# First batch's way into the second attention done row tile by row tile during its gather; value projections moved ahead of the expert phase

## What is computed

```python
x = x + deformable_attention(ctx, norm(x))      # layer 0: 5 sampled keys for each of 16 heads
x = x + experts0(norm(x))                       # 32 experts of width 96, 4 per token
x = x + attention(norm(x), ctx, ctx)            # layer 1: 16 heads of 8, 154 keys, normed, gamma, beta
x = x + experts1(x)                             # 8 experts of width 512, 2 per token, Sinkhorn gate
# attention: probs = softmax(q @ k.T / sqrt(8)); out = probs @ v
```

## Time and profile before

| what | value |
|---|---|
| median of 3 runs | 1001.43 us (1000.84 to 1005.4) |
| the profiled execution's own time | 1003.65 us |
| its span, first to last instruction | 1001.8 us |
| PE busy | 667.4 us, 67% |
| DVE busy | 626.8 us, 63% |
| ACT busy | 423.3 us, 42% |
| POOL busy | 379.5 us, 38% |
| granted TensorE clock, mean | 0.818 |

### The profile page before, as it was taken

One profiled execution on the slowest core, in us unless ns is written; L12 is line 12 of the kernel. 1 busy time (PEld: TensorE's weight loads), 2 busy tenths in 40 slices (PEclk: granted clock), 3 DMA queues, 4 the chain that ended last, 5 costly groups with the idle time before them and its releaser, 6 DMA issues.

```text
span 1001.8 us, 14210 instructions
## 1 busy us (share of the span) xinstructions
PE 667.4 (67%) x3975; PEld 409.8 (41%) x3975; DVE 626.8 (63%) x1579; ACT 423.3 (42%) x906; POOL 379.5 (38%) x345
## 2 busy tenths in 40 slices
PE   5796796687758350777785636787864221799991
PEld 2342352243224240577751313343432111687881
DVE  3678998868948887257533643777754667343443
ACT  2574966665748231344441213354431000344442
POOL 2313223544352388000016886174420000566641
PEclk9998998978979755699995767989865555899996
DMA  4786966554545022244423311000002000111114
GB/s 134 242 280 209 296 223 190 181 169 142 195 158 192 8 82 79 74 127 121 122 75 124 120 43 37 1 17 1 11 1 105 1 0 0 38 43 43 41 35 136
DMA packets 82471, 102.52 MB, mean 102 GB/s; under 512 B 11288, under 2 KB 66014, under 8 KB 82015
## 3 DMA queue, kind: packets, MB, share of 16 engines
q1 hardware_dynamic: 58334, 79.72, 24.9%
q0 software_dynamic: 6592, 13.51, 4.5%
q10 hardware_dynamic: 17472, 8.39, 2.9%
HBM read 81.92 MB, written 19.66 MB: 101 GB/s over the span
## 4 chain that ended last, share of the span: by engine, by line
PE 40%; DVE 29%; ACT 7%; issue 7%; POOL 6%; DMA 5%; another core or an unknown queue 3%; SPq 1%; ACTq 0%; DVEq 0%; POOLq 0%
POOL xs L584 4%; PE PS L1977 4%; DVE oh L1173 3%; PE PS L1955 3%; DVE nmx L1310 3%; PE PS L1960 3%; DMA oh<-index 3%; PE PS L1784 2%; PE PS L1686 2%; PE PS L1858 2%; PE PS L1681 2%; PE PS L1860 2%; PE PS L1886 2%; PE PS L1968 2%
## 5 line engine op out<-in xcount | busy, mean ns | idle before, releaser
L616 POOL DMA_INDIRECT yb<-ys,yrow x64 | 61.2, 956 | 139.7 <-DMA ys<-y 117.7
L584 POOL DMA_INDIRECT xs<-xn,row x64 | 78.1, 1220 | 32.2 <-issue 18.5
L1173 DVE TENSOR_SCALAR oh<-oh,pcol 128x2048 bf16<-128x2048 bf16 x80 | 75.3, 941 | 21.6 <-DMA oh<-index 20.5
L1681 PE MATMUL PS<-oh,T 128*128 128x512 bf16 x240 | 73.2, 418 | 19.7 <-ACT oh L773 19.2
L579 POOL TENSOR_TENSOR vv<-vv,coef 128x1280 f32<-128x1280 f32 x16 | 44.3, 2767 | 97.5 <-DVE coef L1157 88.5
L682 POOL DMA_INDIRECT xg<-xrows,tok x39 | 37.5, 961 | 108.2 <-DVE tok L1519 96.6
L1686 PE MATMUL PS<-oh,T 128*32 128x512 bf16 x960 | 75.3, 421 | 0.3 <-issue 0.3
L1695 PE MATMUL PS<-ident,gs 128*128 128x128 f32 x320 | 56.5, 303 | 26.5 <-ACT vv L794 22.3
L1310 DVE TENSOR_REDUCE nmx<-PS 128x4 f32<-128x616 f32 x64 | 48.9, 794 | 27.9 <-remote 18.5
L786 ACT COPY gs<-PS 128x512 f32<-128x512 f32 x80 | 46.0, 575 | 43.1 <-PE PS L1686 25.4
L772 ACT ACTIVATE oh<-oh,pcol 128x512 bf16<-128x512 bf16 x80 | 57.8, 722 | 14.3 <-DMA oh<-index 14.3
(11 more groups left out here) (372 smaller groups left out, 1777.7 us busy)
## 6 DMA issues: line engine op xcount, KB each, us to landing
oh<-index SPq DMA_DIRECT2D x80, 512.0 KB
oh<-index SPq DMA_DIRECT2D x80, 128.0 KB
x<-xs SPq DMA_DIRECT2D x96, 64.0 KB, 1.9
ys<-y ACTq DMA_DIRECT2D x48, 128.0 KB, 2.2
w0r<-in_w SPq DMA_DIRECT2D x8, 384.0 KB, 5.6
xs<-nil SPq DMA_DIRECT2D x8, 256.0 KB
wg1r<-in_wg SPq DMA_DIRECT2D x1, 2048.0 KB
wu1r<-in_wu SPq DMA_DIRECT2D x1, 2048.0 KB
```

The source lines that it names most:

```text
L584: pool.indirect_dma_start(xs[:], bass.IndirectOffsetOnAxis(ap=row0[:, QT * b + t, k:k + 1], axis=0), xn1[:, b % 2, t, :], None).then_inc(s ...
L616: pool.indirect_dma_start(yb[:, b % 2, t, k, :], None, ys[:], bass.IndirectOffsetOnAxis(ap=yrow0[:, QT * b + t, k:k + 1], axis=0))\
L1173: dve.tensor_scalar(main, main, pcol[:, 0:1], None, ALU.is_equal).then_inc(s["oh_main"], 1)
L1681: pe.matmul(o, T2[:, b % 2, p, n // NK, :], oh[:, slot, GH, :], start=(p == 0), stop=False, skip_group_check=True)
```

## The change

For batch 0 alone, norm, transpose and queries are no longer done once for the batch in slots -11 to -2 but once for each row tile, in a loop that each engine runs ahead of the slots. The loop of DVE takes in the additions of the gather. Each step of the loop works on 128 rows of all four groups: four query matmuls of 128x128, four `qhi`, four `qf`. Between them lie the maxima of groups 0 and 1 for the row tile before. The first score matmul of a group still waits for that group's turn. `x2_ready` is raised for batch 0 where the last tile has been added. The order of the first nine units of maxima is changed (`FIRST_UNITS`), that from the tenth on is not.

The main values of all four batches are made behind sampling, among `keys` 4 to 7, in banks 6 and 4. The tail values of batch 0 are made at pair 1 of the expert phase, and nothing at pair 4; those of batches 1 to 3 stay behind the phase.

```diff
-KV_EVERY, KV_FIRST = 3, 1
+TAIL_PAIR = 1
-KV_KINDS = ("values", "tail_values")
+VALUE_BANKS = (6, 4)
+FIRST_UNITS = [("max", _g, _t) for _t in range(QT) for _g in range(2)] + [("turn", 0, 0)]
+FIRST_UNITS += MAX_UNITS[len(FIRST_UNITS):]
+AHEAD = 2 * QT + 1
...
@@ ScalarE
-                keys((e - E0 // 2) // 4 + 4)
+                i = (e - E0 // 2) // 4 + 4
+                keys(i)
+                values(i - 4)
...
+            def first_rows(t):
+                act.wait_ge(s["var2"], t + 1)
+                logs.link(act.activation(NA.log[:, t:t + 1], NA.var[:, t:t + 1], ACT.Ln))
+                act.activation(NA.rstd[:, t:t + 1], NA.log[:, t:t + 1], ACT.Exp, scale=-0.5).then_inc(s["rs2"], 1)
+                act.wait_ge(s["side_ps"], SIDE["xn2T", 0, t] + 1)
+                act.copy(pnT[:, t * P:(t + 1) * P], PS[:, 4, 0:P]).then_inc(s["side_read"], 1)
...
+                act.wait_ge(s["side_ps"], SIDE["q", 0, t] + 1)
+                for g in range(NG):
+                    cols = slice(g * P, (g + 1) * P)
+                    last = act.activation(qhi[:, t % 2, cols], PS[:, 4, cols], ACT.Identity, bias=bmask[:, 0, g:g + 1], scale=pcol[:, 3:4])
+                last.then_inc(s["q_made"], 1)
...
@@ VectorE
-            for t in range(QT):
+            def first_rows(t):
...
                 dve.wait_ge(s["gathered%d" % t], 16 * K0)
...
+                if t == QT - 1:
+                    dve.sem_inc(s["x2_ready"], 1)
+                c.link(dve.bn_stats(NA.st[:, t, :], XR[:, t, :]))
+                c.link(dve.bn_aggr(NA.mv[:, t, :], NA.st[:, t, :]))
+                dve.tensor_scalar(NA.var[:, t:t + 1], NA.mv[:, t, 1:2], EPS, None, ALU.add).then_inc(s["var2"], 1)
+                dve.wait_ge(s["rs2"], t + 1)
+                dve.tensor_scalar(xn2[:, t, :], XR[:, t, :], NA.mv[:, t, 0:1], NA.rstd[:, t:t + 1], ALU.subtract, ALU.mult)\
+                   .then_inc(s["xn2_ready"], 1)
+
+            def first_queries(t):
+                dve.wait_ge(s["q_made"], t + 1)
+                rows = slice(t * P, (t + 1) * P)
+                for g in range(NG):
+                    cols = slice(g * P, (g + 1) * P)
+                    last = dve.scalar_tensor_tensor(out=qf[:, 0, g, rows], in0=PS[:, 4, cols], scalar=bqk1[:, 0, g:g + 1],
+                                                    in1=qhi[:, t % 2, cols].bitcast(F32), op0=ALU.add, op1=ALU.add)
+                last.then_inc(s["side_read"], 1)
...
-            for r in range(FRONT_FIRST, PERIOD * (B - 1) + BACK_LAST + 1):
+            ahead = list(enumerate(FIRST_UNITS))[0:AHEAD]
+            for t in range(QT):
+                first_rows(t)
+                if t:
+                    maxima(0, ahead[2 * t - 2:2 * t])
+                first_queries(t)
+            maxima(0, ahead[2 * QT - 2:])
+            for r in range(0, PERIOD * (B - 1) + BACK_LAST + 1):
...
@@ TensorE
                     if b == B - 1:
-                        for i in (3, 4, 5):
+                        keys(3)
+                        for i in (4, 5):
                             keys(i)
+                            values(i - 4)
...
             for i in (6, 7):
                 keys(i)
+                values(i - 4)
...
-                if m % KV_EVERY == KV_FIRST and m // KV_EVERY < len(KV_KINDS):
-                    values(0, m // KV_EVERY)
+                if m == TAIL_PAIR:
+                    tail_values(0)
...
+            def first_turn(t):
+                side("xn2T", 0, t)
+                pe.wait_ge(s["xn2_ready"], t + 1)
+                pe.transpose(PS[:, 4, 0:P], xn2[:, t, :], ident[:]).then_inc(s["side_ps"], 1)
+
+            def first_queries(t):
+                pe.wait_ge(s["side_read"], SIDE["xn2T", 0, t] + 1)
+                for g in range(NG):
+                    cols = slice(g * P, (g + 1) * P)
+                    last = pe.matmul(PS[:, 4, cols], wq1[:, cols], pnT[:, t * P:(t + 1) * P], start=True, stop=True)
+                last.then_inc(s["side_ps"], 1)
...
+            for t in range(QT):
+                first_turn(t)
+                if t:
+                    maxima(0, ahead[2 * t - 2:2 * t])
+                first_queries(t)
+            maxima(0, ahead[2 * QT - 2:])
```

More of the change, by code:

```diff
@@ L89, with units_at @@
 MAX_UNITS.append(("turn", NG - 1, 0))
+FIRST_UNITS = [("max", _g, _t) for _t in range(QT) for _g in range(2)] + [("turn", 0, 0)]
+FIRST_UNITS += MAX_UNITS[len(FIRST_UNITS):]
+AHEAD = 2 * QT + 1
+def units_at(b, j):
+    units = MAX_UNITS if b else FIRST_UNITS
+    return [(n, unit) for n, unit in enumerate(units) if n // 2 - 1 == j and (b or n >= AHEAD)]
 MAX_BANKS = (2, 6)
@@ L98 @@
 SIDE = {}
+for _t in range(QT):
+    SIDE["xn2T", 0, _t] = len(SIDE)
+    SIDE["q", 0, _t] = len(SIDE)
 for _r in range(FRONT_FIRST, PERIOD * (B - 1) + BACK_LAST + 1):
@@ L105 @@
         _q = _r - PERIOD * _b
-        if _q == -8:
+        if _b and _q == -8:
             SIDE["xn2T", _b, 0] = len(SIDE)
-        if _q in Q_SLOTS:
+        if _b and _q in Q_SLOTS:
             SIDE["q", _b, Q_SLOTS[_q]] = len(SIDE)
@@ L740, in keys, with values @@
                 last.then_inc(s["k_ev"], 1)
+            def values(b):
+                act.wait_ge(s["v_ps"], b + 1)
+                act.copy(V1[:, b], PS[:, VALUE_BANKS[b % 2], :]).then_inc(s["v_ev"], 1)
             def post(b, n):
@@ L913, in _ @@
                     if q == -10:
-                        deviation(NA, "2", b + 1)
+                        deviation(NA, "2", QT + b)
                     if q == -8:
@@ L1291, in _, with maxima @@
                                                     in1=XR[:, t, :], op0=ALU.mult, op1=ALU.add)
-                    if t < QT - 1 or k < K0 - 1:
-                        c.link(last)
-                if t < QT - 1:
-                    c.tick(dve.bn_stats(NA.st[:, t, :], XR[:, t, :]))
-            last.then_inc(s["x2_ready"], 1)
-            def maxima(b, j):
-                for n, (kind, g, t) in enumerate(MAX_UNITS):
-                    if n // 2 - 1 != j:
-                        continue
+                    c.link(last)
+                if t == QT - 1:
[14 more added lines that the diff above has]
+                last.then_inc(s["side_read"], 1)
+            def maxima(b, units):
+                for n, (kind, g, t) in units:
                     u = N_MAX * b + n
+                    most = nmx if b or g != 1 else nmx1
                     bank = MAX_BANKS[u % 2]
@@ L1321, in split_query @@
                 u = NG * b + g
-                if b == 0:
-                    dve.wait_ge(s["q_made"], g + 1)
-                    dve.scalar_tensor_tensor(out=qf[:, 0, g, :], in0=PS[:, 4, :], scalar=bqk1[:, 0, g:g + 1],
-                                             in1=qhi[:, u % 2, :].bitcast(F32), op0=ALU.add, op1=ALU.add).then_inc(s["side_read"], 1)
-                    return
                 dve.wait_ge(s["side_read"], SIDE["q", b, g] + 1)
@@ L1625, in keys, with values @@
                 last.then_inc(s["k_ps"], 1)
+            def values(b):
+                if b >= 2:
+                    pe.wait_ge(s["v_ev"], b - 1)
+                bank = PS[:, VALUE_BANKS[b % 2], :]
+                pe.matmul(bank, cx[:, b, 1:1 + P], wv1[:], start=True, stop=False)
+                pe.matmul(bank, vrow[:, 1:1 + P], bv1[:], start=False, stop=True).then_inc(s["v_ps"], 1)
             def post(b, n):
@@ L1795, in _ @@
             for b in range(1, B):
-                for n in range(len(KV_KINDS)):
-                    values(b, n)
+                tail_values(b)
             def side(*use):
@@ L1872, in _ @@
                         scores(b, q // 3, q % 3)
[L1873 removed]
+                    maxima(b, units_at(b, q - MAX_FIRST - 1))
                 for b in range(B):
                     q = r - PERIOD * b
[L1876 removed]
+                    if b and q == -8:
                         side("xn2T", b, 0)
[L1878 removed]
+                        pe.wait_ge(s["xn2_ready"], QT + b)
                         for t in range(QT):
@@ L1881, in _ @@
                         last.then_inc(s["side_ps"], 1)
-                    if q in Q_SLOTS:
+                    if b and q in Q_SLOTS:
                         g = Q_SLOTS[q]
```

97 lines of the change are left out of this document (37 added, 60 removed).

## The result

| | before | changed |
|---|---|---|
| median of 20 runs | 1004.23 us (997.22 to 1013.28) | 1011.91 us (1004.23 to 1018.07) |
| ratio to before | | 1.0069, 95% interval 1.0044 to 1.0094 |
| profiled execution, own time | 1003.65 us | 1018.07 us |
| its span | 1001.8 us | 1016.2 us |
| PE, DVE busy | 667.4, 626.8 us | 674.1, 624.2 us |

The change makes the kernel slower by 0.7%, some 7.7 us of the medians. The forecast was +16.7 us, so the direction and the range held, and the forecast size was more than double the measured one. The profiled execution of the changed kernel is the slowest of its 20, so the 14.4 us between the two spans overstate the difference.

The account below looks back on a forecast made before the run. No engine was full; a chain of waits bound it, with POOL's batch 1 gathers behind x2_ready setting slot 1. +17.6 (rounds) - 0.9 (values) = +16.7 us: 1020.3 against the profiled 1003.65, 1018 on the median's scale; range 1007 to 1023.

Parts of the forecast that it names:

- The mechanism: Batch 0 to slot 1: DVE's rounds delay x2_ready, POOL's 30.2 us follow, DVE waits; each us later costs one.
- The gather's loop: DVE's loop over batch 0's tiles: rounds of 9.9, 11.4 and 11.4 us, making x2_ready 17.6 us later.
- 0.28 + 2.01 + 3.0 = 5.3 us: PE's part of a round: one tile's turn 0.28, four maxima matmuls 2.01, four query matmuls with tail 3.0 us.
- The clock: PE in the rounds: granted clock taken as 0.50 throughout; full clock would make the sum about 7 us smaller.
- The rival with the full clock: PE at full clock in the rounds: 6.8 us less, 1011 us; chance 0.2.
- What follows: Behind x2_ready: batch 1 ready at 591.9, slot 1 moves by the full 17.6 us, everything behind in the same order.
- The rival of the long stall: DVE's unexplained 11.24 us idle at 593.73 may vanish in a shifted kernel: 1007 us; chance 0.13.
- The values: Value projections moved behind sampling and to pair 1: expert phase shortened, together -0.9 us.
- The cover behind sampling: Main values delay PE by 2.3 us there, hidden by 7.2 us before the first expert tile: cost nothing.
- worth nothing: Behind the expert phase, beside the gather: three main-value blocks vanish from PE and ACT, with no gain.

Follow-up runs that it names:

- run 3: Changed kernel, but POOL starts batch 1's gathers once batch 0's transfers have landed, awaiting x2_ready only before its last addition: 1010.82 us, ratio 1.0066 to before.
- run 4: Kernel before with POOL's gathers of batch 1 started when batch 0 has landed: 1001.94 us, ratio 0.9989.
- run 7: Changed kernel with DVE's loop reordered, adding each tile as it lands before looking at the previous tile's queries: 1001.85 us, ratio 0.9963 to before.
- run 12: Changed kernel again, unedited, for a second profile: 1008.13 us, ratio 1.0082 to before.
- run 5: Kernel before with batch 2's gathers spaced, pairs each held for a count of mx_used: 991.43 us, ratio 0.9867.
- run 6: Kernel before with batch 2's sixteen gathers kept back to back but held until 16 units of maxima are used: 997.86 us, ratio 0.9942.
- run 1: Kernel before with only the value projections moved as in the change: 1003.08 us, ratio 1.0005.
- run 2: Changed kernel with the value projections back in their old places, the row-tile loop alone: 1019.71 us, ratio 1.0109 to before.
- run 9: Kernel before with gathers of batches 2 and 3 meant to be spaced; twelve of batch 3's sixteen stayed back to back: 985.56 us, ratio 0.9869.
- run 10: Changed kernel with the same spacing edit for gathers of batches 2 and 3: 1001.85 us, ratio 1.0014 to before.

## Why the prediction was right in sign and range, and wrong in size

**The mechanism held.** DVE's additions wait for three other engines, `x2_ready` comes late, POOL's 30.2 us behind it come late, and DVE stands before slot 1's statistics. POOL's part took 591.36 - 561.15 = 30.2 us, to the tenth what the earlier trace rows gave, and it was 30.2 or 30.3 us in every profile but those of runs 3 and 4, while POOL's first gather of batch 1 came anywhere between 16.5 and 38.9 us after the first additions. Run 7 shows that the loss goes when only DVE's order is changed. Run 3, which was meant to take POOL out, doesn't count for it, because a late signal took POOL's place. The first scores moved by 3.8 us and set nothing.

**Step "The gather's loop": the rounds were priced too high.** Forecast were 9.9, 11.4 and 11.4 us, measured 8.75, 10.14 and 9.07, so `x2_ready` moved by 12.9 us and not by 17.6. The terms on DVE and ACT held: additions to the end of the norm 3.1 us (3.2 forecast), four `qhi` 1.5 (1.7 with the hop), four `qf` 1.05 before the next additions (1.2). The error is PE's: 0.28 + 2.01 + 3.0 = 5.3 us forecast. The third round of the changed kernel:

```profile
553.49 0.45 PE L1843 MATMUL PS<-ident,xn 128*128 128x128 f32 x1 [6.95 <-DVE xn L1321]
553.63 1.37 PE L1873 MATMUL PS<-Kbd,qf 128*128 128x308 f32 x4
554.79 1.91 PE L1849 MATMUL PS<-pnT,wq 128*128 128x128 f32 x8
```

From 553.35, the norm's end, to 556.70, the queries' end, it is 3.35 us. This is the term of the sum that was mis-sized, in two parts. Four query matmuls take 1.91 us, 0.48 each. I had priced each at the 0.73 us between two starts in sampling, at the same granted clock of 0.50; why the same shape went slower there no run shows, and that row was the wrong neighbour. And the four maxima matmuls took 1.37 us where I had taken 2.01 from the earlier trace rows. In that row they had begun at 553.21 while the query matmuls before them ran on to 554.20, so 2.01 holds a wait. In the loop each group also began before the one ahead of it was through, where the sum had put them end to end. The second round has 1.1 us more, for ACT got the queries' signal at 547.67 and not at 546.54. POOL's burst for batch 0 ended at 544.6, and this start lies 3.0 us behind it. In run 12 the same signal was 0.85 us late (545.96 for 545.11) and lay 2.7 us behind the burst's end at 543.3. Runs 3, 4 and 7 show the same with longer waits.

**Step "The clock": right.** Granted clock of the changed kernel in the second and third rounds, where PE works and where it waits (columns as in the earlier trace rows):

```profile
543.00:547.00 4.00, 3.19 (x13) 2.93 (x13) 1.70 (x3) 0.27 (x1) 1.34 (x2) 0.50 0.17 39
547.00:553.00 6.00, 0.00 (x0) 0.00 (x0) 3.08 (x12) 1.91 (x6) 0.00 (x0) 0.78 0.00 0
553.00:557.00 4.00, 3.21 (x13) 2.95 (x13) 1.85 (x3) 0.53 (x2) 0.00 (x0) 0.50 0.00 0
```

Where PE works it has 0.50, that is 1.2 GHz. Higher shares fall only into stretches in which it does nothing. The rival with the full clock named 1011 us, close to the result (1011.91), but for a reason that the rows refute, so its closeness is luck. The Trainium skill (TensorE: Matmul & The Clock Gate, HAM oscillation — how this bites in real kernels) describes work in short pieces between waits, each of which starts cold. By that the rounds would be slow because they are rounds; the trace agrees, with 0.50 in each piece. No run here had the same matmuls in one piece to set beside it, and the twelve us of PE's work without a gap in the earlier trace rows had 0.50 too, so the pieces are not shown to be the cause.

**Step "What follows": everything behind slot 1 "is the same" was wrong.** 4.0 us came back in slots 1 to 13 in one profile, 7.7 in the other. The rival of the long stall had seen that the place was fragile, but not its cause: 11.24 us of the earlier trace rows are tied to POOL's burst of batch 2 (runs 5 and 6), which stands behind slot 1 in both kernels. The stall was there in the changed kernel too, in two parts, and why it and the stretch are shorter there stays open:

```profile
605.78 0.80 DVE L1344 TENSOR_REDUCE nmx<-PS 128x4 f32<-128x616 f32 x1 [6.47 <-remote]
...
612.22 0.69 DVE L1341 TENSOR_TENSOR qf<-qf,PS 128x512 fp32r<-128x512 f32 x1 [5.09 <-remote]
```

**Step "The values": -0.9 us, as far as fourteen profiles tell.** The cover behind sampling held. That their removal from the gather is "worth nothing" fits the kernel before (run 1) and was false beside the loop, where it is worth 9.2 us up to slot 1 in the profile of run 2. The sum had silently counted it, because it was worked out with both parts in place.

**Ledger.** Forecast +17.6 - 0.9 = +16.7. Profiles: +12.9 and +12.7 for the rounds, -4.0 and -7.7 given back by slot 13, -0.8 for the values on average, which makes +8.1 and +4.2. Timed: +7.7 us in the medians, +8.6 in run 12's, 1.0069 and 1.0082 as ratios. So 4.7 us of the 9 that were forecast too much are PE's terms in the rounds, and the rest is about what came back by slot 13.

## What to carry to other kernels

Before a loop is cut into pieces so that they start early, look at what the old loop's end released. Here a wait put between two pieces on the releasing engine was paid in full by that second chain up to slot 1, and a faster way to the first consumer was worth only the slack of the second. The order "take in the next piece first, then look at the answer for the last one" kept the early start here without the loss (run 7). Where an idle time has no named cause, look for a burst on another engine that ends with it, and space or move the burst: two lines of waits on POOL were worth 1.3% in run 5, more than the change lost. Then read in the profile whether the burst was spaced at all (run 9).

## What the runs showed of the hardware

- While POOL issued sixteen indirect gathers back to back, signals of finished matmuls came up to some 11 us late (run 3: matmuls ended at 554.91 by the trace, ACT released at 565.67). In the fourteen profiles DVE and ACT have 37 waits of 6 us or more between the first additions and 720 us that are put down to "remote" or "issue". Of these, 21 ended 1.5 to 3.8 us behind the last gather of a burst of fourteen or sixteen (3.1 in run 7, 2.3 in run 3, 3.7 in run 4, 1.5 in run 6), 16 ended while one ran, as that of 6.47 us in the changed kernel did, and none ended anywhere else. Some of the 16 are ordinary waits, such as the 10.68 us of run 2. Spacing the gathers took 11.9 us off the kernel (run 5), moving them moved the stall (run 6). Whether the matmuls or only their signals are late the trace cannot say, because the ends of matmuls in it are modelled. What PE and POOL's transfers share was not found.
- Not every signal is late during a burst. In run 10 the second tile's transpose ended at 541.62 by the trace while batch 0's last gather ran (541.04 to 541.99), and ACT copied it at 541.65. The rounds there took 9.5, 9.1 and 9.1 us.
- The stall of the earlier trace rows was followed by work at the lower clock. Behind the 14.77 us in which PE did nothing before, until 599.06, the granted clock from 599 to 609 us was 0.50; it had been 0.93 from 574.4 to 584.3.
- Single operations of DVE are stretched beside POOL's work: the maxima's small copy took 1.12 us in run 3 where 0.18 is usual, and ended at 580.69, with one of POOL's additions (579.39 to 580.65). A split of 0.75 us took 2.22 in run 6, beside another operation of POOL's (603.63 to 605.52).

```profile
579.57 1.12 DVE L1353 COPY NMp<-nmh 128x16 f32<-128x16 f32 x1
```
